# Two list tiles side by side on 64 rows each of TensorE, three products in place of four

## The reference

```python
x = x + _L0_ffn_ref(_L0_cond_ref(x, ...), ...)
x = x + _L1_ffn_ref(_L1_cond_ref(x, ...), ...)

def _L0_ffn_ref(x, base_w, base_b, A, B, router_w):        # 16 experts, rank 64, 2 of them chosen
    base_out = jnp.einsum('bsi,oi->bso', x, base_w) + base_b
    res_hidden = jnp.einsum('bsi,ri->bsr', x, A)
    probs = softmax(jnp.einsum('bsi,ei->bse', x, router_w))
    topw, topi = top_k(probs, 2); topw = topw / (sum(topw) + 1e-06)
    combine = sum(one_hot(topi, 16) * topw[..., None], axis=-2)
    delta = jnp.einsum('bse,bsr,eor->bso', combine, res_hidden, B)
    return base_out + delta * SCALING
```

## Time and profile before

| | us |
|---|---|
| median of 3 executions | 1298.13 (1295.85 to 1298.81) |
| the profiled execution, its own time | 1295.05 |
| its span on the core | 1293.3 |
| busy: TensorE, VectorE, ScalarE, GpSimd | 1257.1, 645.6, 384.8, 272.5 |
| mean granted TensorE clock | 0.993 |

### The profile page before, as it was taken

The page is one execution under the profiler, slowest core; times in us unless marked ns, Lnnn a source line. Parts: engine busy times, 40 slices in busy tenths (PEclk is TensorE's granted clock), DMA queues, the critical chain, the costliest instruction groups (busy, mean ns, idle before and its releaser), DMA issues.

```text
span 1293.3 us, 22225 instructions
## 1 busy us (share of the span) xinstructions
PE 1257.1 (97%) x7189; PEld 1132.3 (88%) x7189; DVE 645.6 (50%) x1819; ACT 384.8 (30%) x809; POOL 272.5 (21%) x306
## 2 busy tenths in 40 slices
PE   6998999999999999998899999999999999999998
PEld 6998999999899999998678888888888888888887
DVE  6565666766644444445644434335343453453452
ACT  4312222121242433322333333433322222222221
POOL 2222222222122222224211111111122112121100
PEclk9998999999999999999899999999999999999999
DMA  7356767434789888868678899899755545444410
GB/s 276 124 149 231 230 219 235 143 110 129 264 289 330 282 307 298 301 258 211 149 232 267 275 272 293 264 277 309 246 135 102 125 114 96 115 114 97 114 49 33
DMA packets 93602, 260.70 MB, mean 202 GB/s; under 512 B 11649, under 2 KB 32513, under 8 KB 93442
## 3 DMA queue, kind: packets, MB, share of 16 engines
q1 hardware_dynamic: 81024, 221.73, 49.7%
q0 software_dynamic: 11264, 37.76, 16.2%
q10 hardware_dynamic: 1266, 0.70, 0.2%
HBM read 161.58 MB, written 98.57 MB: 201 GB/s over the span
## 4 chain that ended last, share of the span: by engine, by line
PE 50%; DMA 2%; DVE 1%; SPq 0%; issue 0%; ACT 0%; POOL 0%; ACTq 0%; POOLq 0%
PE z L1314 13%; PE z L1316 13%; PE z L1315 13%; PE t L1430 2%; DMA xin<-zs_dram,gpos 2%; PE c L1316 1%; PE c L1314 1%; PE c L1315 1%; PE t L1377 1%; PE t L1378 1%; PE c L1378 1%; PE c L1377 1%; DMA bd<-bd_dram 1%; PE prep L1552 1%; PE prep L1368 0%
## 5 line engine op out<-in xcount | busy, mean ns | idle before, releaser
L1314 PE MATMUL z<-w_1h,yh 128*128 128x384 f32 (+1 forms) x512 | 190.5, 372 | 0.6 <-DVE w_1l L1040 0.6
L1316 PE MATMUL z<-w_1l,yh 128*128 128x384 f32 (+1 forms) x512 | 188.3, 368 | 0.0
L1315 PE MATMUL z<-w_1h,yl 128*128 128x384 f32 (+1 forms) x512 | 188.1, 367 | 0.0
L1314 PE MATMUL z<-w_0h,yh 128*128 128x384 f32 (+1 forms) x512 | 187.7, 367 | 0.0
L1315 PE MATMUL z<-w_0h,yl 128*128 128x384 f32 (+1 forms) x512 | 187.3, 366 | 0.0
L1316 PE MATMUL z<-w_0l,yh 128*128 128x384 f32 (+1 forms) x512 | 187.2, 366 | 0.0
L942 DVE TENSOR_TENSOR yl<-t,yh 128x512 fp32r<-128x512 f32 x128 | 82.3, 684 | 205.1 <-ACT yh L703 205.1
L637 POOL TENSOR_TENSOR carrier<-ones_col 128x1 f32<-128x1 f32 x96 | 20.5, 213 | 701.4 <-DVE den L1013 240.4
L1314 PE MATMUL z<-w_2h,yh 128*128 128x336 f32 (+1 forms) x512 | 153.9, 301 | 9.9 <-DVE den L1013 6.1
L1316 PE MATMUL z<-w_2l,yh 128*128 128x336 f32 (+1 forms) x512 | 152.7, 298 | 0.0
L1315 PE MATMUL z<-w_2h,yl 128*128 128x336 f32 (+1 forms) x512 | 152.7, 298 | 0.0
(11 more groups left out here) (216 smaller groups left out, 2323.8 us busy)
## 6 DMA issues: line engine op xcount, KB each, us to landing
bd<-bd_dram SPq DMA_DIRECT2D x96, 512.0 KB, 5.6
zs_dram<-zt SPq DMA_DIRECT2D x96, 512.0 KB
x8raw<-in_x_dram SPq DMA_DIRECT2D x32, 516.0 KB, 5.5
xin<-in_x_dram SPq DMA_DIRECT2D x32, 512.0 KB
x_dram<-xb SPq DMA_DIRECT2D x32, 512.0 KB, 6.0
out_dram<-xb SPq DMA_DIRECT2D x32, 512.0 KB, 2.9
braw<-in_b_dram SPq DMA_DIRECT2D x32, 256.0 KB
bd_dram<-bd SPq DMA_DIRECT2D x16, 512.0 KB, 2.7
```

Source lines behind the costliest of these rows:

```text
L1314: T.matmul(o, ah, wh, start=start, stop=False, **kw)
L1315: T.matmul(o, al, wh, start=False, stop=False, **kw)
L1316: return T.matmul(o, ah, wl, start=False, stop=stop, **kw)
```

## The change

Every list tile's hidden vector is kept once, 64 numbers. Two list tiles share one `ht` (its left and its right 64 columns), so that one transposition puts the first on rows 0 to 63 and the second on rows 64 to 127 of `hh` and `hl`. B's high and low part lie side by side in the free dimension of `bd` on 64 partitions, the first tile's on partitions 0 to 63, the second's on 64 to 127. `listed_pair` multiplies both tiles, each with matmuls over 64 rows, alternating between the halves and between the banks c and t: three products for each half of the columns (high by high, low by high, high by low) where there were four terms before. What is computed is the same save for the term low by low, which goes away. `split_step` now splits a pair of experts over 128 partitions in one operation each, one pair a step, where it did two experts in two.

In layer 1 the step is reordered: the second pair comes before the transposition of `hx`, `mixing(t + 1)` moves from ahead of that transposition to the middle of `over_y(1)`, and ScalarE copies all four list tiles out ahead of `h1h` and `mixed_out`. Layer 0's step keeps its order.

```diff
-        hs_dram = [scratch(f"hs_dram{w}", [E0 * CAP, 2 * R0]) for w in range(WAVES)]
+        hs_dram = [scratch(f"hs_dram{w}", [E0 * CAP, R0]) for w in range(WAVES)]
         zs_dram = [scratch(f"zs_dram{w}", [LISTED * P, L]) for w in range(WAVES)]
-        bd_dram = scratch("bd_dram", [E0, P, L])
+        bd_dram = scratch("bd_dram", [E0 // 2, 2 * R0, 2, L])
...
-        listed = sb(ctx, "listed", [P, 2, 2, R0])
+        listed = sb(ctx, "listed", [P, 2, R0])
...
-        braw, bd = [], []
-        for v in range(PER):
-            over = ExitStack()
-            braw.append(sb(over, f"braw{v}", [P, L]))
-            over.close()
-            bd.append(sb(ctx, f"bd{v}", [P, L], F32R))
-        ht = [sb(ctx, f"ht{v}", [P, 2 * R0]) for v in range(PER)]
-        hh = sb(ctx, "hh", [P, PER, P], F32R)
-        hl = sb(ctx, "hl", [P, PER, P], F32R)
+        bd = [sb(ctx, "bd0", [2 * R0, 2, L], F32R)]
+        over = ExitStack()
+        braw = [sb(over, f"braw{w}", [2 * R0, L]) for w in range(2)]
+        over.close()
+        bd.append(sb(ctx, "bd1", [2 * R0, 2, L], F32R))
+        ht = [sb(ctx, f"ht{j}", [P, 2 * R0]) for j in range(PER // 2)]
+        hh = sb(ctx, "hh", [2 * R0, PER // 2, P], F32R)
+        hl = sb(ctx, "hl", [2 * R0, PER // 2, P], F32R)
...
+        b0_pair = b0_in_order.rearrange("(p s) r l -> p (s r) l", s=2)
+        bd_of = bd_dram.rearrange("p (s r) k l -> (p s) r k l", s=2)
+
+        def ranks(v):
+
+            return slice(R0 * (v % 2), R0 * (v % 2 + 1))
...
-            def load_b(e, w):
-                for s in range(2):
-                    sp.dma_start(braw[w][R0 * s:R0 * (s + 1), :], b0_in_order[e]).then_inc(b_in[w], 16)
-
-            def store_b(e, w):
-                sp.wait_ge(b_lo, e + 1)
-                sp.dma_start(bd_dram[e], bd[2 + w][:, :].bitcast(F32)).then_inc(bd_out[w], 16)
+            def load_b(p, w):
+                sp.dma_start(braw[w][:, :], b0_pair[p]).then_inc(b_in[w], 16)
+
+            def store_b(p):
+                sp.wait_ge(b_lo, p + 1)
+                sp.dma_start(bd_dram[p], bd[0][:, :, :].bitcast(F32)).then_inc(bd_out, 16)
...
-                    sp.dma_start(ht[v][:, :], hs_t[w][at]).then_inc(ht_in[v], 16)
+                    sp.dma_start(ht[v // 2][:, ranks(v)], hs_t[w][at]).then_inc(ht_in[v], 16)
...
-                sp.dma_start(bd[v][:, :].bitcast(F32), bd_dram[e]).then_inc(bd_in[v], 16)
+                sp.dma_start(bd[v // 2][ranks(v), :, :].bitcast(F32), bd_of[e]).then_inc(bd_in[v], 16)
...
-            def listed_step(s, groups, w, more):
+            def listed_step(s, w, more):
 
                 if more:
                     load_ht(s + 1, w)
-                for group in groups:
+                for group in ((0, 1), (2, 3)):
                     if more:
                         for v in group:
...
-            def split_step(t, more=True):
-
-                for w in range(2):
-                    e = 2 * t - 8 + w
-                    store_b(e, w)
-                    if more:
-                        load_b(e + 2, w)
+            def split_step(t, w, more=True):
+
+                store_b(t - 4)
+                if more:
+                    load_b(t - 2, w)
...
-            def b_high(t, w, first=False):
-
-                act.wait_ge(b_in[w], 32 * t - 32 * 3)
-                if not first:
-                    act.wait_ge(bd_out[w], 16 * t - 16 * 4)
-                copy(bd[2 + w][:, :], braw[w][:, :]).then_inc(b_hi, 1)
+            def b_high(i, w):
+
+                act.wait_ge(b_in[w], 16 * i - 16)
+                if not (at(i, 2) and w == 0):
+                    act.wait_ge(bd_out, 32 * i + 16 * w - 16 * 4)
+                copy(bd[0][:, 0, :], braw[w][:, :]).then_inc(b_hi, 1)
...
-                copy(hh[:, :, :].rearrange("p v r -> p (v r)"), prepp[:, :]).then_inc(hh_ready, 1)
+                copy(hh[:, :, :].rearrange("p j r -> p (j r)"), prepp[:, 0:PER // 2 * P]).then_inc(hh_ready, 1)
...
-                if not last:
-
-                    mixed_out(t + 1)
+                    outputs(s, 2, cp)
+                    outputs(s, 3, tp)
                 act.wait_ge(a1.hT_ps, t + 1)
                 copy(h1h[:, :, :], prepp[0:K1, 0:2 * P].rearrange("p (k r) -> p k r", r=P)).then_inc(a1.hT_hi, 1)
-                if lists:
-                    outputs(s, 2, tp)
-                    outputs(s, 3, cp)
                 if not last:
+
+                    mixed_out(t + 1)
                     y_high(a1, t + 1, 0)
                     y_high(a1, t + 1, 1)
                 if turn is not None:
...
-                V.tensor_tensor(listed[:, :, :, :].rearrange("p k a r -> p (k a) r"),
-                                z[2][:, SM0:SM0 + R0].unsqueeze(1).to_broadcast([P, 4, R0]),
-                                w22[:, :, :].rearrange("p k a -> p (k a)").unsqueeze(2).to_broadcast([P, 4, R0]),
-                                ALU.mult).then_inc(listed_ready, 1)
+                V.tensor_tensor(listed[:, :, :], z[2][:, SM0:SM0 + R0].unsqueeze(1).to_broadcast([P, 2, R0]),
+                                w12[:, :].unsqueeze(2).to_broadcast([P, 2, R0]), ALU.mult).then_inc(listed_ready, 1)
...
-                q = slice(R0, P)
-                dve.wait_ge(b_hi, 2 * t - 8 + w + 1)
-                V.tensor_tensor(bd[2 + w][q, :], braw[w][q, :], bd[2 + w][q, :], ALU.subtract).then_inc(b_lo, 1)
+                dve.wait_ge(b_hi, t - 3)
+                V.tensor_tensor(bd[0][:, 1, :], braw[w][:, :], bd[0][:, 0, :], ALU.subtract).then_inc(b_lo, 1)
...
-            def over_y(b, wh, wl, stop=False, pieces=None):
-
-                for k in range(KC):
+            def over_y(b, wh, wl, stop=False, pieces=None, chunks=range(KC)):
+
+                for k in chunks:
...
-                for v in range(PER):
-                    mm = T.transpose(prepp[:, P * v:P * (v + 1)], ht[v][:, :], ident[:, :])
+                for j in range(PER // 2):
+                    mm = T.transpose(prepp[:, P * j:P * (j + 1)], ht[j][:, :], ident[:, :])
                 mm.then_inc(ht_ps, 1)
 
-            def listed_product(s, v, banks):
+            def listed_pair(s, j):
 
                 pe.wait_ge(hl_ready, s + 1)
-                pe.wait_ge(bd_in[v], 16 * s + 16)
+                for v in (2 * j, 2 * j + 1):
+                    pe.wait_ge(bd_in[v], 16 * s + 16)
                 for half in range(2):
                     w = slice(HALF * half, HALF * (half + 1))
-                    T.matmul(banks[half][:, :], hh[:, v, :], bd[v][:, w], start=True, stop=False)
-                    mm = T.matmul(banks[half][:, :], hl[:, v, :], bd[v][:, w], start=False, stop=True)
-                mm.then_inc(zt_ps, 1)
+                    for v, o in ((0, cp), (1, tp)):
+                        T.matmul(o[half][:, :], hh[ranks(v), j, :], bd[j][ranks(v), 0, w], start=True, stop=False)
+                    for v, o in ((0, cp), (1, tp)):
+                        T.matmul(o[half][:, :], hl[ranks(v), j, :], bd[j][ranks(v), 0, w], start=False, stop=False)
+                    for v, o in ((0, cp), (1, tp)):
+                        mm = T.matmul(o[half][:, :], hh[ranks(v), j, :], bd[j][ranks(v), 1, w], start=False, stop=True)
+                        if half:
+                            mm.then_inc(zt_ps, 1)
...
-                    listed_product(s, 0, cp)
-                    listed_product(s, 1, tp)
+                    listed_pair(s, 0)
...
-                    pe.wait_ge(zt_out, PER * s + 1)
-                    listed_product(s, 2, cp)
                     pe.wait_ge(zt_out, PER * s + 2)
-                    listed_product(s, 3, tp)
+                    listed_pair(s, 1)
...
-                    listed_product(s, 0, cp)
-                    listed_product(s, 1, tp)
+                    listed_pair(s, 0)
                 if first:
                     pe.wait_ge(a0.z_out[0], TILES)
                 else:
                     pe.wait_ge(a1.z_out[0], t)
                 over_y(0, w1h, w1l, pieces=w1_lo[0] if first else None)
                 if lists:
-                    pe.wait_ge(zt_out, PER * s + 1)
-                if not last:
-                    mixing(t + 1)
+                    pe.wait_ge(zt_out, PER * s + 2)
+                    listed_pair(s, 1)
                 pe.wait_ge(a1.hx, 2 * t + 2)
                 for k in range(2):
                     mm = T.transpose(prepp[0:K1, P * k:P * (k + 1)], hx1[:, K1 * k:K1 * (k + 1)], ident[:, :])
                 mm.then_inc(a1.hT_ps, 1)
                 if tiles:
                     list_tables(1)
-                if lists:
-                    pe.wait_ge(zt_out, PER * s + 2)
-                    listed_product(s, 2, tp)
                 if first:
                     pe.wait_ge(a0.z_out[1], TILES)
                 else:
                     pe.wait_ge(a1.z_out[1], t)
-                over_y(1, w1h, w1l, pieces=w1_lo[1] if first else None)
+                over_y(1, w1h, w1l, pieces=w1_lo[1] if first else None, chunks=range(KC // 2))
```

(12 more changed lines are left out.)

46 lines of the change are left out of this document (21 added, 25 removed).

## The result

The changed kernel takes 1284.57 us (median of 4 runs, 1283.24 to 1286.09) against 1297.74 for the kernel before, a ratio of 0.990 with a 95% interval of 0.988 to 0.992. Timed again unaltered beside other kernels it took 1289.08 (6 runs, 1284.36 to 1290.80), ratio 0.9935 (0.991 to 0.996). The two differences of medians are 13.2 and 7.1 us (1296.20 before in the second comparison), so I take the gain as 7 to 13 us, where 5.2 was forecast. The one profile of the changed kernel (its own time 1286.09, span 1284.2) lies 9.1 under that of before, span by span, and that is the difference I take apart.

The account below looks back on a forecast made before the run. The prediction took TensorE, busy 1257.1 of 1293.3 us, to bound the kernel. Its terms, −5.2 + 1.9 − 3.8 + 1.4 + 0.5 = −5.2 us, took the median from 1298.13 to 1292.9, range 1284 to 1314.

Parts of the forecast that it names:

- the forecast's own case: Whole kernel: the summed terms hold, 1292.9 us, bounds 1289 to 1298; chance 0.45.
- the first rival: Bursts of 64-row products: the two halves load side by side, saving 0.11 us a burst, −5.3, about 1288; chance 0.15.
- the products, +1.9: Steps with lists: six paired slots plus 0.20 us per row change, 1.91 a burst against 1.87; +1.9 us in all.
- Transpositions, −5.2: Transpositions of the lists: two in place of four in each of 24 steps, 0.109 us each; −5.2 us.
- The split, −3.8: Split of B, layer 0 steps 4 to 11: x8l 1.4 us earlier, `den` waits 1.2 and 1.2 shorter; bounds 0 and −6.
- The last term, 1.2 for steps 6 to 11: Split of B: a third of the other `den` waits, 3.5 us in three places, is won; 1.2 us.
- Step 0 of layer 1, +1.4: Step 0 of layer 1: six matmuls that stood within mixing's wait now stand behind it, 0.233 us each; +1.4 us.
- The reorder elsewhere, 0: Layer 1's other steps: the new order costs nothing; bounds −1 and +5 us.
- Start of wave 1's lists, +0.5: Wave 1's first lists: both bd needed 2.45 us earlier, loads issued about 1.25 earlier; +0.5 us, bounds −0.5 and +3.

Follow-up runs that it names:

- experiment 3: The changed kernel with each burst of twelve matmuls cut in two of six, three 128-row matmuls of `over_y` between them: 1306.12 us, ratio 1.008.
- experiment 10: The changed kernel with 32 unused bytes behind `hl` and `b_low` done in two subtractions of 64 partitions: 1284.76 us, ratio 0.991.
- experiment 5: The changed kernel with each pair of experts loaded into `braw` by two transfers of 64 partitions, not one of 128: 1284.99 us, ratio 0.9915.
- experiment 4: The changed kernel with step 0 of layer 1 alone in the old order: 1283.28 us, ratio 0.990.
- experiment 1: The kernel before with only the changed kernel's order of layer 1's step, products as before: 1298.53 us, ratio 1.0015.
- experiment 2: The changed kernel with all three products of c, then all three of t, in each half of the columns: 1284.94 us, ratio 0.991.

## Why the prediction was right, and where it was off

The direction, the mechanism and the range (1284 to 1314) held, the time at its lower end. 5.2 us were forecast, 9.1 came in the profile and 7 to 13 between medians. The first comparison and the profile lie below the forecast's own case (1289 to 1298, given 0.45), the second comparison (1289.08) at its edge; the bursts are those of the first rival, the two halves loading side by side (about 1288, given 0.15). The term that was mis-sized most is that of the products, +1.9, which measured −3.0.

- **Transpositions, −5.2.** Right: with two in place of four `turn_ht` is 0.22 shorter (0.17 in place of 0.39 to the next matmul in layer 0, 0.14 in place of 0.36 in layer 1), in 24 steps.
- **Products, +1.9.** Right in the halves side by side, in the slot of 0.233 and in the 0.20 a change (0.19 by experiment 3). Wrong in "the second half's first load trails the first's by another 0.11": both loads stand at 692.97. With the addresses out of the way (experiment 10), a step with lists gains 0.30 in layer 0 and 0.43 in layer 1, 0.22 of it the transpositions; the rest, 12 × 0.08 + 12 × 0.21 = 3.0 us, is the two bursts (why it is less in layer 0 wasn't looked for). So the term was −3.0 and not +1.9, and the first rival, with 0.15, had it nearly (−3.4). The Trainium skill ("TensorE: Matmul & The Clock Gate", Part 3) has this right: different row groups load and start together, here within 0.01 us.
- **The split, −3.8.** −2.9 and −2.1 measured, with the addresses' +0.07 a step in it, so −5.5 without them. From the turn on, x8l came 1.5 earlier (1.4 forecast) and `den` another 1.26 (1.2 forecast). The first is right, though the layout of the load is worth less than that by itself (experiment 5). The second is right by luck: the prediction read the earlier trace rows as two subtractions of 2.2 and took what was left of the wait, but one takes 1.22, and the rest of the 4.43 was the wait for GpSimd's add, which the changed kernel has too. The wait for `den` did not shrink (2.77, under 0.5 forecast). TensorE was faster between the two waits than I had thought of, its granted clock 1.00 over the 24 matmuls of `conv`, 3.14 us, where before it was 0.63 and they took 4.60. The last term, 1.2 for steps 6 to 11, was 2.1 (2.5 without the addresses' 0.07 a step), and its reason was incomplete: the second subtraction counts there only beside a late add of GpSimd (experiment 10).

```profile
107.10:111.70 4.60, 4.60 (x24) 4.40 (x24) 4.57 (x3) 1.45 (x3) 2.10 (x1) 0.63 0.29 80
```

```profile
106.14:109.28 3.14, 3.13 (x24) 2.92 (x24) 3.14 (x2) 0.50 (x2) 2.09 (x1) 1.00 0.00 0
```

(stretches of the kernel before, then of the changed one)

- **Step 0 of layer 1, +1.4.** +1.6 in the profile, +1.7 with the order alone, both inside a scatter of 7 us from profile to profile (experiment 4): in agreement, not shown.
- **The reorder elsewhere, 0.** Right: 23.41 and 19.27 in experiment 1.
- **Start of wave 1's lists, +0.5.** −0.8 here: the wait for bd grew from 1.52 to 2.85, and one of 1.61 for ht went away. But the interval from step 2 to 3 was 23.7 to 28.7 in the twelve profiles without an additional load, and nothing so small can be read from one.
- **Not forecast:** the addresses, +2.5; the granted clock behind a wait, +1.4 in the step from 18 to 19; and the scatter where a gather or a list's first load is waited for. Steps 0 to 3 of layer 1 took 77.2 us in the first profile of the changed kernel and 80.6 in the second, and 69.7 in that of experiment 5.

The terms add up: −5.2 − 3.0 − 5.5 + 1.6 − 0.8 + 2.5 + 1.4 = −9.0, of 9.1 measured. The medians show 13.2 in the first comparison because the profiled execution of before lies 2.7 under its median and that of the changed kernel 1.5 over its own. Such scatter goes with the clock: in one set of 17 executions of the kernel before, the fastest (1294.56) had a mean granted clock of 0.993 and the slowest (1303.58) of 0.988.

## What to carry to other kernels

Two products over 64 rows really share the array, and need not be written in turn, but each passage between 64 and 128 rows costs 0.19 us: count the passages before the slots, since 22 us of saved slots shrank to 3 here. After any change of a buffer's size compare the pitch of matmuls that weren't touched; 32 unused bytes were worth nearly as much (2.5 us) as the products (3.0). Where an instruction of VectorE is recorded longer than its like, look at what GpSimd does beside it before pricing it. And read the share of the DMA with the GB/s beside it, and test its room with a transfer more, since 0.99 was not full and yet not free.

## What the runs showed of the hardware

- The first matmul of one half of the rows starts with the first of the other half even where three of the other stand ahead of it in the program (experiment 2).
- Matmuls of 384 columns start 0.173 us apart with the weights (the moving operand; yh and yl lie ahead of hl and didn't move) 32 bytes above a multiple of 64 (w0_0h at byte 136160 before), and 0.175 with them at a multiple of 64 (132288 with the change). Those of 512 columns start 0.233 apart either way. Why, the runs don't tell.
- With bd loaded into 64 partitions a transfer in place of 128, a step took 1.8 to 2.0 us more of the DMA's share for 2.1 MB, and TensorE waited for bd only once, at the start of wave 1, as before the change.
- A subtraction over 1024 fp32 columns takes 1.22 us on VectorE for 64 or 128 partitions. When it starts while GpSimd's add over 128 x 1024 (2.4 us) runs, it ends 1.08 to 1.14 after that add: the 4.43 that the profile of before gave for two in a row holds such a wait.
- The granted clock over the 4 to 5 us behind a wait of TensorE was 0.63 after 2.77 (before), 0.62 after 2.77 (changed) and 0.50 after 4.13 (experiment 10) in step 5, and 0.66 after 2.59 in the changed kernel's step 18. It was 1.00 after 1.26, but also after 2.44 (before) and 2.82 (experiment 10) in step 18.
